# One attention kernel for a perceiver block: the value product cut into four quarters among the score chunks, with a wait on each quarter's own cast

## The chip, the cores and the metric

The kernel runs on one NeuronCore of one Trainium2 chip. The metric is the device time of one execution in microseconds (us). Engines: PE (TensorE) multiplies matrices into PSUM, DVE (VectorE) and ACT (ScalarE) read PSUM and SBUF, POOL (GpSimd) works on SBUF, SP (SyncE) here only issues transfers.

## The reference, cut to what matters

The whole block is a cross-attention with quantised operands, a self-attention and a mixture of experts, each added to `x`. The change touches the cross-attention alone. With 16 heads of 16 columns, 4,096 queries and 8,192 keys it computes

```python
q = _fq_sym(q * scale, axis=-1); k = _fq_sym(k, axis=-1); v = _fq_sym(v, axis=2)   # 8-bit grids
attn = jnp.einsum('bhqd,bhkd->bhqk', q, k)
attn = jax.nn.softmax(attn.astype(jnp.float32), axis=-1)
attn = _fq_unsigned(attn, axis=-1)          # round to 255 steps of the row's maximum
out = jnp.einsum('bhqk,bhkd->bhqd', attn, v)
```

`_fq_unsigned` divides by the row's maximum over 255, rounds, and multiplies back, so what reaches the value product are integers from 0 to 255, and a factor for each row.

## The kernel before, in words

**Units.** A unit `u` is one head and one tile of 128 queries against all 8,192 keys: 16 heads x 32 tiles = 512 units. Four units (`TG = 4`, `t` = 0 to 3) of the same head are what the code calls a head `i`: there are `HEADS` = 128 such heads. A head shares one set of keys and values and one PSUM tile `pO`.

**A unit's way through the engines.**
1. PE multiplies queries by keys into PSUM, in five chunks of 4, 3, 4, 3, 2 banks (even `t`) or 3, 4, 3, 4, 2 banks (odd `t`) of 512 columns (`scores`, L834 to L843). There are only two PSUM buffers, `ring0` and `ring1`, used in turn. The chunks with number 2 and 4 have two more matmuls ahead (L838), which are written over.
2. DVE copies each chunk to SBUF, scaled, and takes its minimum (L914: `D0` to `D4`), then reduces five minima to the bias of the exponential (L921: `BIAS`).
3. ACT takes the exponential of four pieces of 2,048 keys into 8-bit integers (L973: `E0` to `E3`).
4. SP issues a transposing transfer for each piece (L733), which brings `n_op` to `pairs`.
5. POOL casts each transposed piece to 16-bit floats, `nT` (L789, `unpack`).
6. PE multiplies `nT` by the values into `pO`, 64 matmuls of 128 columns (L853, `value_product`), done two periods after the unit's scores were read.

**What closes a head.** In the second period (`t` = 1) of the next head ACT copies the finished `pO` to `oT` (L997, `OC`), PE folds four row groups of `oT` back into `pO` (L861, `FOLD`), and in the third period (`t` = 2) ACT scales the folded result into `att_g` (L991, `FIN`, semaphore `s_fin`). The first value product of the new head writes to `pO` again, and so waits for `s_fin`: it is that of unit `t` = 0 and stands in period `t` = 2.

**What sets the order.** Each engine runs a list of steps for each period, written by hand (L645 to L647); a period `u` of PE holds chunks 2 to 4 of unit `u + 1` (`M2` to `M4`), chunks 0 and 1 of unit `u + 2` (`N0`, `N1`) and the value product of unit `u - 2` (`AV`). An engine carries out its instructions in the order of its list. Every `M` and `N` waits until DVE has emptied its PSUM buffer (`s_mu`), and DVE waits for the chunk (`s_m`). The order on ACT is `DEN E0 FIN E1 OC E2 E3`, on DVE `D0 BIAS D1 D2 D3 INV D4`, with `DEN`, `INV`, `OC`, `FOLD` at `t` = 1 and `FIN` at `t` = 2 only. In DVE's period `u`, `D0` to `D4` are the five copies of unit `u + 1`; PE's `M2` can start when `D0` is done, `M3` when `D1` is, `M4` when `D2` is, `N0` when `D3` is and `N1` when `D4` is. The semaphores that the change touches are `s_un` (a cast is done, counted four to a unit) and `s_av` (a value product is done, counted once a unit before).

Of the kernel before, what the change touches and what calls it, by code (L numbers as in the profile page):

```python
# [28 lines left out]
def build(nc, a, out):  # L29
    NT = a["x"].shape[0] * a["x"].shape[1]  # L30
    NK = a["ctx_T"].shape[1]
    QT, KT = NT // P, NK // P
    UNITS = H * QT
# [5 lines left out]
    TG = 4  # L39
# [11 lines left out]
    with top:  # L51
# [12 lines left out]
        def sem(name, ctx=top):  # L64
            return ctx.enter_context(nc.semaphore(name))
# [32 lines left out]
        with nc.Block() as block:  # L98
            @block.sync
            def _(sp):  # L100
                def weights(dst, src, s):
                    sp.dma_start(dst[:], src.rearrange("(c p) n -> p c n", p=P)).then_inc(s, 16)
                weights(wkv_sb, a["L0_xattn_Wkv"], s_wkv)
                sp.wait_ge(s_zero, 1)
                for r in range(PARTS):
                    sp.dma_start(b_all[32 * r:32 * r + 1, 0:2 * D],
                                 a["L0_xattn_bkv"].rearrange("(a n) -> a n", a=1)).then_inc(s_bkv, 16)
                    sp.dma_start(b_all[32 * r:32 * r + 1, 2 * D:3 * D],
                                 a["L0_xattn_bq"].rearrange("(a n) -> a n", a=1)).then_inc(s_bkv, 16)
# [529 lines left out]
        NE = 4  # L639
        EW = NK // NE  # L640
        EK = KT // NE
        EP = EK // 2
        PAIRS = KT // 2
        HEADS = NG * H
        PE_STEPS = "M2 M3 AV0 M4 AV1 N0 N1 FOLD".split()  # L645
        DVE_STEPS = "D0 BIAS D1 D2 D3 INV D4".split()
        ACT_STEPS = "DEN E0 FIN E1 OC E2 E3".split()  # L647

# [37 lines left out]
        s_un = sem("integers_unpacked", xs)  # L686
        s_av = sem("value_product_done", xs)
# [9 lines left out]
        def scored(u, j):  # L697
            return u * NM + j + 1

        def exped(u, j):  # L700
            return u * NE + j + 1

        def ge(e, s, value):

            if not isinstance(value, int) or value > 0:
                e.wait_ge(s, value)
# [12 lines left out]
        def exists(u):  # L719
            return not isinstance(u, int) or 0 <= u < UNITS  # L720

        with nc.Block() as block:
# [19 lines left out]
            @block.gpsimd  # L742
            def _(pool):
                def load_keys(g, h, b):
                    cols = bass.ds(g * TG * P, TG * P)
                    pool.dma_start(k_op[b][0:KR, :], kT_d[h * KR:(h + 1) * KR, :]).then_inc(s_k[b], 16)
                    for r in range(PARTS):
                        pool.dma_start(q_op[b][r * HD:(r + 1) * HD, :], qT_d[h * HD:(h + 1) * HD, cols]  # L748
                                       ).then_inc(s_qh[b], 16)

                def load_values(h, b):
                    pool.dma_start(v_st[b][:], v_d[h]).then_inc(s_v[b], 16)

                def stage_steps(g, h):
                    nc.gpsimd.tensor_copy(step[h % 2][:], q_step[:, bass.ds(g * TG + h * QT, TG)]).then_inc(s_st, 1)

                def stage_values(b):
                    nc.gpsimd.tensor_copy(v_op[b][:, :, 0:HD], v_st[b][:].rearrange("p (k d) -> p k d", d=HD)
                                          ).then_inc(s_vo, 1)

                def values(i, b, h, more):
                    pool.wait_ge(s_v[b], (i + 2 - b) * 8)
                    ge(pool, s_av, (i - 1) * TG)
                    pool.sem_inc(s_turn, 1)
                    stage_values(b)
                    if more:
                        pool.wait_ge(s_vo, i + 1)
                        pool.sem_inc(s_turn, 1)
                        load_values((h + 2) % H, b)

                def keys(g, h, i):
                    pool.wait_ge(s_mu, scored((i - 2) * TG + TG - 1, NM - 1))
                    stage_steps(g, h)
                    load_keys(g, h, h % 2)

                def store(g):
                    pool.wait_ge(s_fin, (g + 1) * H)
                    pool.sem_inc(s_turn, 1)
                    pool.dma_start(att_d[bass.ds(g, 1)].rearrange("a p t d -> (a p) t d"), att_g[:]).then_inc(s_as, 16)

                def unpack(u, t, j):
                    par = t % 2
                    pool.wait_ge(s_n[par][j], (u + 2 - par) * 8)
                    if j == 0:
                        ge(pool, s_av, u - 1)
                    pool.sem_inc(s_turn, 1)
                    src = pairs[par][:, j * EP:(j + 1) * EP, :].rearrange("p a b -> p (a b)").bitcast(U8).rearrange(
                        "p (a b c) -> p a c b", c=2, b=P)
                    nc.gpsimd.tensor_copy(nT[par][:, j * EK:(j + 1) * EK, :].rearrange("p (a c) b -> p a c b", c=2), src  # L789
                                          ).then_inc(s_un, 1)  # L790

                def head(g, h, i):
                    for t in range(TG):
                        u = i * TG + t
                        unpack(u, t, 0)
                        if t == 3 and exists(u + 2 * TG):
                            keys(g + (h + 2) // H, (h + 2) % H, i + 2)
                        unpack(u, t, 1)
                        if t == 3 and h == 0 and exists(u - H * TG):
                            store(g - 1)  # L800
                        unpack(u, t, 2)
                        unpack(u, t, 3)
                        if t == 1 and (not isinstance(i, int) or 2 <= i + 1 < HEADS):
                            values(i + 1, (h + 1) % 2, (h + 1) % H, exists(u + 3 * TG))

                for b in range(2):
                    nc.gpsimd.memset(v_op[b][:], 0.0).then_inc(s_init, 1)
                stage_steps(0, 0)
                stage_steps(0, 1)
                pool.wait_ge(s_pad, 2)  # L810
                load_keys(0, 0, 0)
                load_values(0, 0)
                load_keys(0, 1, 1)
                load_values(1, 1)
                pool.wait_ge(s_init, 2)
                for b in range(2):
                    pool.wait_ge(s_v[b], 16)
                    stage_values(b)
                for b in range(2):
                    pool.wait_ge(s_vo, b + 1)  # L820
                    load_values(2 + b, b)
                for h in range(H):
                    head(0, h, h)
                with pool.Fori(1, NG - 1) as g:
                    for h in range(H):
                        head(g, h, g * H + h)
                for h in range(H):
                    head(NG - 1, h, (NG - 1) * H + h)
                store(NG - 1)
                pool.wait_ge(s_as, 16 * NG)  # L830

            @block.tensor
            def _(pe):
# [8 lines left out]
                                              k_op[b][:, at + n * BANK:at + (n + 1) * BANK], start=True, stop=True)  # L842
                    mm.then_inc(s_m, 1)  # L843

                def value_product(u, i, b, t, half):

                    if half == 0:
                        pe.wait_ge(s_un, (u + 1) * NE)
                    if half == 0 and t == 0:
                        pe.wait_ge(s_vo, i + 1)  # L850
                        ge(pe, s_fin, i)
                    for n in range(half * KT // 2, (half + 1) * KT // 2):
                        mm = nc.tensor.matmul(pO[32 * (n % CG):32 * (n % CG) + 32, t, :], v_op[b][:, n, :],  # L853
                                              nT[t % 2][:, n, :], start=n < CG, stop=n >= KT - CG)
                    if half == 1:
                        mm.then_inc(s_av, 1)

                def fold_groups(i):
                    pe.wait_ge(s_oc, i + 1)
                    for t in range(TG):  # L860
                        mm = nc.tensor.matmul(pO[:, t, 0:HD], oT[:, t, :], fold[:], start=True, stop=True)  # L861
                    mm.then_inc(s_of, 1)

                def period(i, hp, t):
                    u = i * TG + t
                    for x in PE_STEPS:
                        if x[0] in "MN":
# [31 lines left out]
                    for t in range(TG):  # L899
                        period(HEADS - 2 + hp, hp, t)  # L900
                for t in range(TG - 2, TG):
                    for half in range(2):
                        value_product(UNITS - TG + t, HEADS - 1, 1, t, half)
                fold_groups(HEADS - 1)

            @block.vector
# [57 lines left out]
            def _(act):  # L964
# [27 lines left out]
                    last.then_inc(s_fin, 1)  # L992

                def copy_products(i):
                    act.wait_ge(s_av, i * TG + TG)
                    ge(act, s_of, i)
                    nc.scalar.copy(oT[:], pO[:]).then_inc(s_oc, 1)  # L997

# [534 lines left out]
        NE = a["member"].shape[0] // PARTS  # L1533
# [297 lines left out]
```

## Time and profile before

| | |
|---|---|
| Three executions | 6421.8, 6457.5 and 7106.4 us, median 6457.5 us |
| The profiled execution | 6431.7 us, span of its trace 6430.2 us |
| Stage of the cross-attention (first to last chunk of scores) | some 340 to 5,190 us of the span |
| Busy over the whole span | DVE 87%, ACT 74%, POOL 71%, PE 70% |

What comes ahead of and behind that stage (keys, values and queries; then projection, self-attention and experts) is not touched by the change.

### The profile page before, as it was taken

To read this page: it belongs to the slowest core of one execution; us is meant where nothing else is said; L and a number is where in the kernel's file an instruction comes from. 1 tells how busy PE (TensorE), PEld (TensorE's weight loads), DVE (VectorE), ACT (ScalarE), POOL (GpSimd) and SP (SyncE) were. 2 spreads that over 40 slices of the span, in tenths; PEclk is the share of its full clock that TensorE was granted. 3 is DMA by queue.
4 is the path that set the end of the run, shared out by engine and by line. 5 is a ranking of instruction groups with operands and counts; after the bars stand their busy time and mean duration, and the time that the engine had idled before them with its cause. 6 is when DMAs were issued, how large, how long until landed. Compare 5 with 4: busy or idle time off the path is not lost. (4 is left out here: it accounts for less than half of the span.)

```text
span 6430.2 us, 141911 instructions
## 1 busy us (share of the span) xinstructions
PE 4487.4 (70%) x48939; PEld 2136.5 (33%) x49654; DVE 5619.6 (87%) x7587; ACT 4772.4 (74%) x6550; POOL 4588.0 (71%) x3259
## 2 busy tenths in 40 slices
PE   7556666666666666666666666666666646769999
PEld 3322222222222222222222222232222233455555
DVE  8799999999999999999999999999999936872222
ACT  5479998998999899989999988989989933331111
POOL 4578888888898888888888888888888823420000
PEclk9899999999999999999999999999999978979999
DMA  4267777777777777777777777777777730010000
GB/s 127 76 123 139 140 142 146 139 144 142 142 143 141 143 139 141 142 140 140 142 142 145 139 138 139 147 140 141 145 141 141 138 87 0 0 36 4 7 8 9
DMA packets 2231984, 735.80 MB, mean 114 GB/s; under 512 B 2175781, under 2 KB 2209416, under 8 KB 2225577
## 3 DMA queue, kind: packets, MB, share of 16 engines
q1 hardware_dynamic: 2196265, 576.08, 44.0%
q0 software_dynamic: 35456, 157.33, 13.8%
q14 instruction: 234, 1.92, 0.1%
q8 instruction: 29, 0.48, 0.0%
HBM read 168.97 MB, written 27.26 MB: 31 GB/s over the span
## 5 line engine op out<-in xcount | busy, mean ns | idle before, releaser
L914 DVE TENSOR_SCALAR_CACHE_REDUCE scores<-ring,step 128x2048 f32<-128x2048 f32 (+2 forms) x2560 | 4780.0, 1918 | 50.5 <-PE ring L841 38.1
L973 ACT ACTIVATE n_op<-scores,bias 128x2048 uint8<-128x2048 f32 x2048 | 4076.2, 1997 | 284.6 <-DVE m_rest L921 284.5
L789 POOL CAST nT<-pairs 128x2048 f16<-128x2048 uint8 x2048 | 3791.1, 1890 | 510.9 <-DMA pairs<-n_op 491.4
L841 PE MATMUL ring<-x_all,q_op 128*128 128x512 bf16 x7746 | 2147.6, 385 | 702.2 <-DVE scores L914 630.5
L841 PEld LDWEIGHTS ring<-x_all,q_op 128*128 128x128 bf16 x8192 | 682.2, 98 | 1854.1 <-DVE scores L914 1180.6
L838 PE MATMUL ring<-x_all,q_op 128*128 128x512 bf16 x1793 | 571.9, 389 | 775.2 <-DVE scores L914 744.1
L853 PE MATMUL pO<-nT,v_op 128*32 128x128 f16 x32768 | 659.0, 223 | 141.0 <-ACT att_g L991 109.0
L853 PEld LDWEIGHTS pO<-nT,v_op 128*32 128x32 f16 x32768 | 481.6, 98 | 590.2 <-issue 512.2
L838 PEld LDWEIGHTS ring<-x_all,q_op 128*128 128x128 bf16 x2048 | 116.7, 97 | 997.8 <-DVE scores L914 979.4
L973 ACT ACTIVATION_READ_ACCUMULATOR n_op<-scores,bias 128x1 f32 x2048 | 396.1, 193 | 0.0
L1752 DVE TENSOR_TENSOR h_up<-h_gate,pUp 128x512 f32<-128x512 f32 x112 | 76.9, 687 | 298.8 <-ACT h_gate L1741 298.8
L1741 ACT ACTIVATE h_gate<-pGt 128x512 f32<-128x512 f32 x112 | 66.8, 597 | 337.7 <-PE pWt L1715 337.6
L1342 POOL TENSOR_TENSOR k_bd<-kT,head_mask 128x512 f32<-128x512 f32 x128 | 129.3, 1042 | 166.7 <-ACT kT L1442 166.7
L997 ACT COPY oT<-pO 128x512 f32<-128x512 f32 x128 | 74.9, 585 | 221.9 <-PE pO L853 221.9
L1712 PE MATMUL pGt<-zT,wg_sb 128*128 x448 | 223.0, 620 | 2.8 <-DVEq L1747 2.8
L1712 PE MATMUL pUp<-zT,wu_sb 128*128 x448 | 211.1, 594 | 0.0
L914 DVE DVE_READ_ACCUMULATOR scores<-ring,step 128x1 f32 x2560 | 209.3, 82 | 0.0
L1724 PE MATMUL pDn<-wd_sb,hidden 128*128 128x256 f32 (+1 forms) x896 | 195.6, 380 | 0.0
L748 POOL DMA_DIRECT2D q_op<-queries_transposed x384 | 188.6, 495 | 2.0 <-issue 1.8
L1724 PEld LDWEIGHTS pDn<-wd_sb,hidden 128*128 128x128 f32 (+1 forms) x896 | 169.5, 190 | 24.8 <-issue 1.8
L1768 DVE TENSOR_TENSOR x_all<-x_all,pDn 128x256 f32 x32 | 13.5, 421 | 169.6 <-PE pDn L1724 169.6
L1741 ACT ACT_TABLE_LOAD x8 | 10.3, 1283 | 200.6 <-PE pWt L1715 200.6
(202 smaller groups left out, 3616.1 us busy)
## 6 DMA issues: line engine op xcount, KB each, us to landing
x_all<-keys_transposed POOLq DMA_DIRECT2D x128, 768.0 KB, 8.5
v_st<-value_integers POOLq DMA_DIRECT2D x128, 256.0 KB, 3.5
pairs<-n_op SPq DMA_TRANSPOSE x2048, 2.8
keys_transposed<-kT_s POOLq DMA_DIRECT2D x32, 384.0 KB, 3.3
cT<-in_ctx_T SPq DMA_DIRECT2D x32, 256.0 KB, 2.6
x_all<-in_x SPq DMA_DIRECT2D x2, 4096.0 KB, 16.2
q_op<-queries_transposed POOLq DMA_DIRECT2D x384, 16.0 KB, 8.4
value_integers<-v_int SPq DMA_DIRECT2D x1, 4096.0 KB, 13.0
```

The source lines that it names most:

```text
L748: pool.dma_start(q_op[b][r * HD:(r + 1) * HD, :], qT_d[h * HD:(h + 1) * HD, cols]).then_inc(s_qh[b], 16)
L789: nc.gpsimd.tensor_copy(nT[par][:, j * EK:(j + 1) * EK, :].rearrange("p (a c) b -> p a c b", c=2), src).then_inc(s_un, 1)
L838: nc.tensor.matmul(slot(t, j)[:, n * BANK:(n + 1) * BANK], q_op[b][:, t * P:(t + 1) * P], k_op[b][:, at + n * BANK:at + (n + 1) * BANK], s ...
L841: mm = nc.tensor.matmul(slot(t, j)[:, n * BANK:(n + 1) * BANK], q_op[b][:, t * P:(t + 1) * P], k_op[b][:, at + n * BANK:at + (n + 1) * BAN ...
L853: mm = nc.tensor.matmul(pO[32 * (n % CG):32 * (n % CG) + 32, t, :], v_op[b][:, n, :], nT[t % 2][:, n, :], start=n < CG, stop=n >= KT - CG)
L914: nc.vector.tensor_scalar(score[t % 2][:, at:at + width * BANK], slot(t, j)[:, 0:width * BANK], step[b][:, t:t + 1], None, ALU.mult, ALU.m ...
L973: nc.scalar.activation(n_op[par][:, j * EW:(j + 1) * EW], score[par][:, j * EW:(j + 1) * EW], ACT.Exp, bias=bias[par][:], scale=-1.0, accu ...
L1342: nc.gpsimd.tensor_tensor(k_bd[i][:, c, b], kT[i][:, c, b * B:(b + 1) * B].unsqueeze(1).to_broadcast([P, HC, B]), head_mask[:].unsqueeze(2 ...
L1712: nc.tensor.matmul(dst[0:r, :], w[:, c, cols], zT[:, c, bass.ds(blk * TB, TB), :].rearrange("p t n -> p (t n)"), start=c == 0, stop=c == D ...
L1724: mm = nc.tensor.matmul(pDn[t % 2], hidden[0:rows[f], f, t * P:(t + 1) * P], wd_sb[0:rows[f], f, :], start=f == 0, stop=f == NF - 1)
L1741: nc.scalar.activation(h_gate[f % 2][0:rows[f], :], pGt[f % 2][0:rows[f], :], ACT.Silu).then_inc(s_si, 1)
L1752: nc.vector.tensor_tensor(h_up[i][0:rows[f], :], h_gate[i][0:rows[f], :], pUp[i][0:rows[f], :], ALU.mult).then_inc(s_hu, 1)
```

## The change

The value product of a unit is cut into four quarters of 16 matmuls (16 of 64 key tiles) instead of two halves of 32, and PE's list of steps puts one quarter behind each of `M2`, `M3`, `M4` and `N0`. Each quarter waits for the cast of its own piece, where before the first half waited for all four casts. Each quarter adds one to `s_av`, so all thresholds on `s_av` are multiplied by four. Each cast now waits for the quarter of unit `u - 2` that read the same piece of the same buffer, where before only the first cast waited, for the whole product of `u - 2`. The wait for `s_fin` and for the staged values stays with the first quarter of unit `t` = 0.

```diff
-        PE_STEPS = "M2 M3 AV0 M4 AV1 N0 N1 FOLD".split()
+        PE_STEPS = "M2 AV0 M3 AV1 M4 AV2 N0 AV3 N1 FOLD".split()
...
-                    ge(pool, s_av, (i - 1) * TG)
+                    ge(pool, s_av, (i - 1) * TG * NE)
...
-                    if j == 0:
-                        ge(pool, s_av, u - 1)
+                    ge(pool, s_av, exped(u - 2, j))
...
-                def value_product(u, i, b, t, half):
-
-                    if half == 0:
-                        pe.wait_ge(s_un, (u + 1) * NE)
-                    if half == 0 and t == 0:
+                def value_product(u, i, b, t, j):
+                    pe.wait_ge(s_un, exped(u, j))
+                    if j == 0 and t == 0:
                         pe.wait_ge(s_vo, i + 1)
                         ge(pe, s_fin, i)
-                    for n in range(half * KT // 2, (half + 1) * KT // 2):
+                    for n in range(j * EK, (j + 1) * EK):
                         mm = nc.tensor.matmul(pO[32 * (n % CG):32 * (n % CG) + 32, t, :], v_op[b][:, n, :],
                                               nT[t % 2][:, n, :], start=n < CG, stop=n >= KT - CG)
-                    if half == 1:
-                        mm.then_inc(s_av, 1)
+                    mm.then_inc(s_av, 1)
...
-                    act.wait_ge(s_av, i * TG + TG)
+                    act.wait_ge(s_av, (i * TG + TG) * NE)
```

The lines of the kernel after are up to four lower than before: L838, L841, L853 and L861 of PE become L837, L840, L850 and L857, and L997 of ACT becomes L993.

**PE in the third period of a head (`t` = 2).** The rows below are PE's instructions from the fold to chunk `N0`, in the kernel before; the names in brackets are semaphores waited for (`head_finished` is `s_fin`, `scores_copied` is `s_mu`, `integers_unpacked` is `s_un`).

```order
L861 MATMUL pO<-fold,oT 128x16 x3
L838 MATMUL ring<-x_all,q_op 128x512 [waits scores_copied]
L841 MATMUL ring<-x_all,q_op 128x512 x3
L841 MATMUL ring<-x_all,q_op 128x512 [waits scores_copied]
L841 MATMUL ring<-x_all,q_op 128x512 x3
L850 REGISTER_ALU [waits integers_unpacked]
L853 MATMUL pO<-nT,v_op 32x128 [waits head_finished,head_values_staged]
L853 MATMUL pO<-nT,v_op 32x128 x31
L838 MATMUL ring<-x_all,q_op 128x512 [waits scores_copied]
```

The same place in the kernel after:

```order
L857 MATMUL pO<-fold,oT 128x16 x3
L837 MATMUL ring<-x_all,q_op 128x512 [waits scores_copied]
L840 MATMUL ring<-x_all,q_op 128x512 x3
L847 REGISTER_ALU [waits integers_unpacked]
L850 MATMUL pO<-nT,v_op 32x128 [waits head_finished,head_values_staged]
L850 MATMUL pO<-nT,v_op 32x128 x15
L840 MATMUL ring<-x_all,q_op 128x512 [waits scores_copied]
L840 MATMUL ring<-x_all,q_op 128x512 x3
L850 MATMUL pO<-nT,v_op 32x128 [waits integers_unpacked]
```

The matmul that waits for `head_finished` has moved from behind chunk `M3` (the second row of L841 with a wait) to ahead of it.

**PE in the second period of a head (`t` = 1).** The rows below are PE's instructions from chunk `M4` to the fold, before:

```order
L838 MATMUL ring<-x_all,q_op 128x512 [waits scores_copied]
L841 MATMUL ring<-x_all,q_op 128x512 x2
L853 MATMUL pO<-nT,v_op 32x128 x32
L841 MATMUL ring<-x_all,q_op 128x512 [waits scores_copied]
L841 MATMUL ring<-x_all,q_op 128x512 x2
L841 MATMUL ring<-x_all,q_op 128x512 [waits scores_copied]
L841 MATMUL ring<-x_all,q_op 128x512 x3
L861 MATMUL pO<-fold,oT 128x16 [waits head_products_copied]
```

and after:

```order
L837 MATMUL ring<-x_all,q_op 128x512 [waits scores_copied]
L840 MATMUL ring<-x_all,q_op 128x512 x2
L850 MATMUL pO<-nT,v_op 32x128 [waits integers_unpacked]
L850 MATMUL pO<-nT,v_op 32x128 x15
L840 MATMUL ring<-x_all,q_op 128x512 [waits scores_copied]
L840 MATMUL ring<-x_all,q_op 128x512 x2
L850 MATMUL pO<-nT,v_op 32x128 [waits integers_unpacked]
L850 MATMUL pO<-nT,v_op 32x128 x15
L840 MATMUL ring<-x_all,q_op 128x512 [waits scores_copied]
L840 MATMUL ring<-x_all,q_op 128x512 x3
L857 MATMUL pO<-fold,oT 128x16 [waits head_products_copied]
```

The last matmuls of the value product stood ahead of chunk `N0` before and stand behind it now, between `N0` and `N1`.

## Rows read from the trace of the kernel before

**Rows 1.** Busy time by stretch: us, PE, PEld, DVE, ACT, POOL, PEclk, DMA share, GB/s.

```profile
1000.00:5000.00 4000.00, 2701.13 (x35921) 1173.60 (x36503) 3964.76 (x5199) 3606.16 (x4777) 3525.87 (x2446) 0.99 0.74 142
```

**Rows 2.** The page's costliest groups, DVE's copy of a chunk with its idle time.

```profile
L914 DVE TENSOR_SCALAR_CACHE_REDUCE scores<-ring,step 128x2048 f32<-128x2048 f32 (+2 forms) x2560 | 4780.0, 1918 | 50.5 <-PE ring L841 38.1
```

**Rows 3.** Waits over the whole span: total us, times, longest us.

```profile
ACT oT L997 <- PE pO L853: 221.9, 128, 7.4
PE pO L853 <- ACT att_g L991: 109.0, 126, 1.3
```

**Rows 4.** Waits between 1000 and 5000 us: total us, times, longest us.

```profile
PE pO L853 <- ACT att_g L991: 90.6, 105, 1.3
DVE scores L914 <- PE ring L841: 24.7, 46, 3.1
PE pO L853 <- POOL nT L789: 13.9, 10, 3.8
DVE scores L914 <- ACT n_op L973: 8.6, 5, 1.8
POOL nT L789 <- PE pO L853: 5.8, 6, 2.5
```

**Rows 5.** Timeline of DVE, copies of one head's period t = 2.

```profile
2521.71 1.81 DVE L914 TENSOR_SCALAR_CACHE_REDUCE scores<-ring,step 128x1536 f32<-128x1536 f32 x1
...
2523.44 2.35 DVE L914 TENSOR_SCALAR_CACHE_REDUCE scores<-ring,step 128x2048 f32<-128x2048 f32 x1
...
2525.72 1.28 DVE L914 TENSOR_SCALAR_CACHE_REDUCE scores<-ring,step 128x1024 f32<-128x1024 f32 x1
```

**Rows 6.** Timeline of PE in the same head, periods t = 1 and t = 2.

```profile
2515.72 0.63 PE L853 MATMUL pO<-nT,v_op 128*32 128x128 f16 x32
2516.49 0.82 PE L841 MATMUL ring<-x_all,q_op 128*128 128x512 bf16 x3
...
2519.94 0.81 PE L841 MATMUL ring<-x_all,q_op 128*128 128x512 bf16 x3
2521.85 1.04 PE L841 MATMUL ring<-x_all,q_op 128*128 128x512 bf16 x4 [1.10 <-DVE scores L914]
2523.74 0.63 PE L853 MATMUL pO<-nT,v_op 128*32 128x128 f16 x32 [0.86 <-ACT att_g L991]
2524.30 0.60 PE L838 MATMUL ring<-x_all,q_op 128*128 128x512 bf16 x2
```

**Rows 7.** Timeline of ACT in the same head.

```profile
2516.40 0.58 ACT L997 COPY oT<-pO 128x512 f32<-128x512 f32 x1 [1.60 <-PE pO L853]
2516.88 2.00 ACT L973 ACTIVATE n_op<-scores,bias 128x2048 uint8<-128x2048 f32 x1
...
2522.85 0.75 ACT L991 ACTIVATE att_g<-pO,rden 128x16 f32<-128x16 f32 x4
```

**Rows 8.** Timeline of POOL in the same head.

```profile
2510.93 15.03 POOL L789 CAST nT<-pairs 128x2048 f16<-128x2048 uint8 x8 [0.35 <-DMA pairs<-n_op]
2525.92 1.03 POOL L758 COPY v_op<-v_st 128x1024 f16<-128x1024 f16 x1
```

**Rows 9.** Timeline of PE ahead of and in two stretches of low clock.

```profile
2160.08 0.60 PE L838 MATMUL ring<-x_all,q_op 128*128 128x512 bf16 x2 [2.50 <-DVE scores L914]
...
2162.43 1.89 PE L841 MATMUL ring<-x_all,q_op 128*128 128x512 bf16 x4 [0.75 <-DVE scores L914]
...
3203.51 1.04 PE L841 MATMUL ring<-x_all,q_op 128*128 128x512 bf16 x4 [1.10 <-DVE scores L914]
3205.40 1.04 PE L853 MATMUL pO<-nT,v_op 128*32 128x128 f16 x32 [0.86 <-ACT att_g L991]
```

**Rows 10.** Busy time by stretch of 1 us, columns as in the first group.

```profile
3204.00:3205.00 1.00, 0.55 (x3) 0.05 (x1) 1.00 (x1) 1.00 (x6) 1.00 (x1) 1.00 1.13 258
...
3206.00:3207.00 1.00, 1.00 (x21) 0.46 (x11) 1.00 (x1) 1.00 (x1) 1.00 (x1) 0.50 1.14 258
```

**Rows 11.** Timeline of DVE, copies that waited for PE behind those stretches.

```profile
2164.36 2.35 DVE L914 TENSOR_SCALAR_CACHE_REDUCE scores<-ring,step 128x2048 f32<-128x2048 f32 x1 [0.25 <-PE ring L841]
...
3208.31 1.28 DVE L914 TENSOR_SCALAR_CACHE_REDUCE scores<-ring,step 128x1024 f32<-128x1024 f32 x1 [0.85 <-PE ring L841]
...
3210.07 2.35 DVE L914 TENSOR_SCALAR_CACHE_REDUCE scores<-ring,step 128x2048 f32<-128x2048 f32 x1 [0.47 <-PE ring L841]
```

More of the change, by code:

```diff
@@ L901, in _ @@
                 for t in range(TG - 2, TG):
-                    for half in range(2):
-                        value_product(UNITS - TG + t, HEADS - 1, 1, t, half)
+                    for j in range(NE):
+                        value_product(UNITS - TG + t, HEADS - 1, 1, t, j)
                 fold_groups(HEADS - 1)
```

## The prediction

> **What bounds the kernel now.** I read the busy times by stretch first. Between 1000 and 5000 us, deep in the cross-attention, DVE is busy 3964.8 of 4000 us (99.1%), ACT 3606.2 (90%), POOL 3525.9 (88%), PE 2701.1 (68%) [rows 1]. DVE sets the pace; its copies of score chunks stand one behind the other. Its whole idle time ahead of them is 50.5 us in the span [rows 2]. So whatever the change saves on another engine can return at most some 50 us (0.8%), while each microsecond for which DVE lacks a chunk is added to the time in full.
>
> The waits come next, for the places where PE isn't waiting for DVE. In 4000 us PE waited 13.9 us for casts and 90.6 us, in 105 waits, for ACT's last step of the previous head [rows 4]. That second wait is the one to look at: over the span it comes 126 times, 109.0 us in total, 0.87 us each, at most 1.3 [rows 3], so in practically each head after the first, of the same length each time. Today it costs nothing, and the timeline shows why. In one head ACT's FIN starts at 2522.85 and ends at 2523.60 [rows 7], and the value product of unit t = 0 starts at 2523.74 after 0.86 us of idle PE [rows 6]. The chunk ahead of it, M3, had been written from 2521.85 on [rows 6], while DVE copied M2's (2521.71 to 2523.44), so DVE took M3's at 2523.44 without a gap [rows 5].
>
> **The change, part by part.**
>
> *Each quarter waits for its own cast.* PE's waits for casts are 13.9 us of 4000 [rows 4], and they lie in PE's free time. In the head shown eight casts (units t = 0 and t = 1) run from 2510.93 to 2525.92, so the four of unit t = 0 end near 2518.4 [rows 8], and its product starts at 2523.74: a margin of 5.3 us. Cost and gain zero; what hides it is DVE's queue of copies. Were this cover gone, the price would be the 13.9 us.
>
> *Each cast waits for its quarter.* The casts waited 5.8 us for products [rows 4]. POOL has three more waits a unit, with the later casts and behind them SP's transfers queued after each. The quarters of u - 2 are issued within one period and the casts of u follow later, so I take zero. POOL is idle 12% of the stretch, which is 4.5 us in a head of some 38 us (4000/105).
>
> *Splitting the products.* 32 matmuls take 0.63 us [rows 6], so there are as many matmuls as before, in four portions of at most 0.4 us. In periods without the FIN wait a portion lies between two chunks, where PE idles 1 us or more on DVE (1.10 us ahead of M3 [rows 6]). Nothing on the path. What relief it brings ahead of N0 is bounded by DVE's 24.7 us of waits for PE [rows 4].
>
> *The last quarter moves behind N0.* In period t = 1 the product ended at 2515.72 + 0.63 = 2516.35 and ACT's copy OC of `pO` started at 2516.40, having waited 1.60 us for it [rows 6, 7]. Now the last quarter follows N0, which starts at 2516.49, since it needs DVE's D3, and takes 0.82 [rows 6]: 2517.31. A value product directly behind a chunk begins about when the chunk ends; sixteen matmuls take between half of 0.63 and 0.4, I take 0.33. So the product ends at 2517.64 and OC starts at 2517.69, **1.29 us later**. Queued behind OC on ACT are E2, E3, E0 of the next unit and FIN. Before, FIN ended 2523.60 - 2516.40 = 7.20 us after OC's start, with no idle time between [rows 7]. So FIN now ends at 2524.89.
>
> *The first quarter moves ahead of M3.* PE's order is fixed, so M3 now queues behind the quarter that waits for FIN. M2 ends at 2519.94 + 0.81 = 2520.75; PE then stands still until the quarter starts at 2524.89 + 0.14 = 2525.03 (the 0.14 is 2523.74 - 2523.60 [rows 6, 7]), that is 4.28 us. The quarter takes 0.33, M3 starts at 2525.36 and with its 1.04 us ends at 2526.40. DVE takes it 0.04 us later, as 2164.36 follows 2162.43 + 1.89 [rows 9, 11]. DVE would start D3 at 2526.44 instead of 2523.44: **3.00 us lost in each head**. M4, next, has its 2.28 us (2523.44 to 2525.72 [rows 5]) under D3; it needs some 0.3 for the second quarter and 1.0 for itself, so nothing more is lost. In the next head ACT waits for DVE's bias again at t = 1 and OC for PE, so the loss repeats: 127 heads x 3.00 = 381 us.
>
> *PE's clock.* PE stands still for 4.3 us in each head, longer than the idle times at which its clock fell before. At 3203.51 to 3205.40 it had waited 1.10 us, written M3 and waited 0.86 us [rows 9]; then the granted clock went from 1.00 (2.4 GHz) to 0.50 (1.2 GHz) [rows 10], and DVE lost 0.85 + 0.47 = 1.32 us [rows 11]. After an idle 2.50 us at 2160 the same came, and a chunk of four took 1.89 us instead of 1.04 [rows 9]. Where the low clock meets M3, the loss is that difference, 0.85 us; it is then hidden partly behind D3's 2.28 us. Bounds: 0 (no fall, or before M3) and 1.70 (two chunks lengthened, each by 0.85). I take 0.85 in each head, since the idle stretch ends exactly at M3: 127 x 0.85 = 108 us.
>
> The Trainium skill bears on this (TensorE: Matmul & The Clock Gate, section on HAM oscillation): a kernel that idles on a wait between bursts of matmuls can start each burst at the low clock, and pays at every repetition. By its figures of 426.7 and 215.7 ns for a matmul of 512 columns at the two levels, M3 would grow by 0.84 us, an estimate of 107 us in 127 heads. Rows so far show the fall only now and then, since the idle times were shorter.
>
> **The sum.** 6431.7 (the profiled execution) + 381 + 108 = 6921 us, say **6920**. The profiled execution lies 0.4% under the median of the three shown, 6457.5, and by it the change is +7.6%.
>
> **The rivals.**
> - *The stall alone, without a lower clock.* 6431.7 + 381 = 6813 us. For it: a clock of 0.99 in the stage [rows 1]. Against it: falls after shorter idle times [rows 9, 10].
> - *OC is not later.* If ACT's copy came when it did before, FIN would end at 2523.60, M3 would start at 2523.74 + 0.33 = 2524.07, DVE would get it at 2525.15, 1.71 us late: 127 x 1.71 = 217, giving 6649 us. Against it: OC waited 221.9 us in 128 heads for PE [rows 3], so it follows PE.
> - *Slow clock that costs more.* 3.00 + 1.70 = 4.70 us in each head, 597 us, 7029 us.
> - *Not slower: FIN comes in time.* DVE loses nothing if M3 is written by 2523.40, so the quarter must start by 2523.40 - 1.04 - 0.33 = 2522.03 and FIN end by 2521.9, that is 3.0 us earlier than I work out and 1.7 earlier than in the trace of before. ACT would have to get OC that much earlier, and it waits for PE there. Then only relief is left: 6431.7 less at most 50.5 [rows 2], 6381 to 6432 us, no change by measure.
>
> **How the numbers follow.** Stall with low clock 0.54 (6920), stall alone 0.24, costlier clock 0.09, OC not later 0.07, not slower 0.05, and 0.01 for a gain over 2%, for which no row speaks. The range goes down to the stall alone less all of DVE's present idle time, 6813 - 50 = 6763, say 6765, and up to 7029, say 7030. About 2% is what a measurement of this kernel can tell from no change; all cases but the last two lie beyond it, so slower has 0.94, within 2% 0.05, faster 0.01.
>
> **What the changed profile would show.** DVE waits for PE at its copies, one wait of 3 to 4 us a head, some 400 to 500 us in all where 38.1 stood. PE waits for ACT's FIN some 127 times, about 4.3 us each instead of 0.87, directly ahead of the quarter, with M3 behind it. OC on ACT starts right after the quarter behind N0. A head takes 41 to 42 us, and DVE's busy share falls to about 90%. PE's granted clock is 0.5 right after the stall in most heads if the clock term is right, near 1 if the stall-alone rival is. The forecast is wrong if the wait for FIN stays near 0.9 us, or if DVE's copies stay without gaps while PE waits.

## The result, and the profile after

The kernel after takes 6932.4 us (median of four, 6931.3 to 6939.7), the kernel before 6445.7 (median of three, 6421.8 to 6457.5; a fourth execution, at 7106.4 us, was disturbed and is left out). The ratio is 1.076, 95% interval 1.0725 to 1.0803: 7.6% slower. Over the 13 to 20 runs of before that stand beside each group of experiments its median is 6436 to 6442 us, and the terms below are taken against 6440. A difference between experiments of different groups can be off by those 5 us.

The profiled execution of after has a span of 6938.2 us. The stretch from 1000 to 5000 us in it (columns as in rows 1):

```profile
1000.00:5000.00 4000.00, 2606.54 (x32465) 1102.58 (x33039) 3597.41 (x4711) 3273.80 (x4322) 3212.00 (x2216) 0.93 0.66 128
```

DVE is busy 89.9% of it, where it was 99.1% [rows 1], and PE's mean granted clock is 0.93 where it was 0.99. The work hasn't grown; DVE has gaps. The page's group of DVE's copies says how much and behind what:

```profile
L910 DVE TENSOR_SCALAR_CACHE_REDUCE scores<-ring,step 128x2048 f32<-128x2048 f32 (+2 forms) x2560 | 4789.9, 1918 | 549.8 <-PE ring L840 537.9
```

Idle time ahead of the copies is 549.8 us instead of 50.5 [rows 2], 499 us more, which is the lengthening within 2%. The waits over the whole span (total us, times, longest):

```profile
PE pO L850 <- ACT att_g L987: 545.3, 127, 4.3
...
DVE scores L910 <- PE ring L840: 537.9, 160, 11.1
```

PE waits for FIN 127 times as before, but 4.29 us each instead of 0.87 [rows 3]. In one head PE's timeline shows M2 (2502.89), the standstill, the first quarter and M3 behind it:

```profile
2502.89 0.81 PE L840 MATMUL ring<-x_all,q_op 128*128 128x512 bf16 x3
2508.00 0.51 PE L850 MATMUL pO<-nT,v_op 128*32 128x128 f16 x16 [4.29 <-ACT att_g L987]
2508.44 1.89 PE L840 MATMUL ring<-x_all,q_op 128*128 128x512 bf16 x4
```

ACT's timeline in the same head has OC, which waits longer for the product than the 1.60 us of before [rows 7], and FIN:

```profile
2500.65 0.59 ACT L993 COPY oT<-pO 128x512 f32<-128x512 f32 x1 [2.90 <-PE pO L850]
...
2507.11 0.75 ACT L987 ACTIVATE att_g<-pO,rden 128x16 f32<-128x16 f32 x4
```

and DVE's has the gap ahead of its copy of M3's chunk, where it had none [rows 5]:

```profile
2510.36 2.35 DVE L910 TENSOR_SCALAR_CACHE_REDUCE scores<-ring,step 128x2048 f32<-128x2048 f32 x1 [3.88 <-PE ring L840]
```

Last, the clock around the standstill (columns as in rows 1, the granted clock is third from the right):

```profile
2507.00:2508.00 1.00, 0.00 (x2) 0.04 (x2) 0.00 (x0) 1.00 (x7) 1.00 (x1) 1.00 0.76 169
2508.00:2509.00 1.00, 1.00 (x18) 0.52 (x19) 0.00 (x0) 1.00 (x1) 0.92 (x2) 0.58 0.51 117
2509.00:2510.00 1.00, 1.00 (x4) 0.15 (x1) 0.00 (x0) 1.00 (x3) 1.00 (x1) 0.50 0.65 145
```

PE stands still at 1.00, and the clock falls to 0.50 (1.2 GHz) as the quarter and M3 begin. So M3 takes 1.89 us instead of 1.04. The pattern repeats in each head; this one's OC comes again 41.27 us later, at 2541.92.

This head is one of the cheaper ones, since the clock fell during its quarter. From 1000 to 5000 us the trace shows 96 quarters behind such a wait; 84 of them ran wholly at the low clock (0.61 or 0.62 us), and DVE's usual gap is 4.0 us. One such head, in PE's and DVE's timelines:

```profile
2590.65 0.62 PE L850 MATMUL pO<-nT,v_op 128*32 128x128 f16 x16 [4.29 <-ACT att_g L987]
2591.20 1.89 PE L840 MATMUL ring<-x_all,q_op 128*128 128x512 bf16 x4
...
2593.13 2.35 DVE L910 TENSOR_SCALAR_CACHE_REDUCE scores<-ring,step 128x2048 f32<-128x2048 f32 x1 [3.99 <-PE ring L840]
```

### The profile page after: what moved, and what is told of

The parts are those of the page before. It is cut to its first block and busy times, and to the rows that moved or that the text cites. A ratio compares the mean times of both kernels' runs of the same rounds, so it can differ in the third digit from the quotient of the medians.

```text
span 6938.2 us, 144882 instructions
## 1 busy us (share of the span) xinstructions
PE 4711.2 (68%) x48877; PEld 2191.9 (32%) x49654; DVE 5630.6 (81%) x7587; ACT 4782.8 (69%) x6550; POOL 4612.0 (66%) x3259
## 3 DMA queue, kind: packets, MB, share of 16 engines
q14 instruction: 242, 1.97, 0.1%
## 5 line engine op out<-in xcount | busy, mean ns | idle before, releaser
L910 DVE TENSOR_SCALAR_CACHE_REDUCE scores<-ring,step 128x2048 f32<-128x2048 f32 (+2 forms) x2560 | 4789.9, 1918 | 549.8 <-PE ring L840 537.9
L840 PE MATMUL ring<-x_all,q_op 128*128 128x512 bf16 x7560 | 2198.3, 401 | 523.2 <-DVE scores L910 440.7
L850 PE MATMUL pO<-nT,v_op 128*32 128x128 f16 x32768 | 891.1, 233 | 556.9 <-ACT att_g L987 545.3
L837 PE MATMUL ring<-x_all,q_op 128*128 128x512 bf16 x1917 | 625.3, 403 | 822.3 <-DVE scores L910 802.4
L840 PEld LDWEIGHTS ring<-x_all,q_op 128*128 128x128 bf16 x8192 | 704.9, 101 | 1321.0 <-DVE scores L910 542.5
L850 PEld LDWEIGHTS pO<-nT,v_op 128*32 128x32 f16 x32768 | 512.2, 100 | 1503.3 <-issue 1298.4
L837 PEld LDWEIGHTS ring<-x_all,q_op 128*128 128x128 bf16 x2048 | 118.3, 99 | 1070.0 <-DVE scores L910 1044.5
L993 ACT COPY oT<-pO 128x512 f32<-128x512 f32 x128 | 75.1, 587 | 374.6 <-PE pO L850 374.6
L1764 DVE TENSOR_TENSOR x_all<-x_all,pDn 128x256 f32 x32 | 13.5, 421 | 169.6 <-PE pDn L1720 169.6
```

The source lines that it names most:

```text
L837: nc.tensor.matmul(slot(t, j)[:, n * BANK:(n + 1) * BANK], q_op[b][:, t * P:(t + 1) * P], k_op[b][:, at + n * BANK:at + (n + 1) * BANK], s ...
L840: mm = nc.tensor.matmul(slot(t, j)[:, n * BANK:(n + 1) * BANK], q_op[b][:, t * P:(t + 1) * P], k_op[b][:, at + n * BANK:at + (n + 1) * BAN ...
L910: nc.vector.tensor_scalar(score[t % 2][:, at:at + width * BANK], slot(t, j)[:, 0:width * BANK], step[b][:, t:t + 1], None, ALU.mult, ALU.m ...
```

## The experiments

Theory: the FIN wait now stands ahead of M3 and comes later, and PE's standstill brings on a low clock that lengthens M3. The rivals: only the place of the wait counts; the low clock costs nothing of its own; or finer waits and smaller portions cost the time. All edits but one are to the kernel after. Where steps of PE differ by period, the loop takes `PE_AT.get(t, PE_STEPS)` in place of `PE_STEPS`.

### The place of the wait

```diff
+        PE_AT = {2: "M2 M3 AV0 AV1 M4 AV2 N0 AV3 N1 FOLD".split()}
```

> The changed kernel, with one chunk moved in the third period of a head only (t = 2): PE's steps are M2 M3 AV0 AV1 M4 ..., so M3 no longer queues behind the wait for FIN. The last quarter stays behind N0 at t = 1, so FIN still ends 1.29 us late. Theory (queue behind the FIN wait): M3 is on time, but two quarters stand between the FIN wait and M4. They start at 2525.03 on the clock of the head of before and take 0.66, M4 with its two extra matmuls 1.0, so D4 is 0.95 us late in each head: 127 x 0.95 = 121 us, some 6555 us; with a low clock behind the now shorter stand of PE (2.1 us) up to 0.9 us more a head, 6670. Rival (the finer waits or the splitting themselves cost the time): stays near 6930. Rival (moving the FIN wait is everything, the late OC nothing): back to 6430 to 6450.

Measured: 6723.3 us, ratio to before 1.0442 (1.0419 to 1.0465). M3 no longer queues, and 209 us come back, but the time is 53 us above the upper end expected. DVE's gaps differ from head to head. In one head:

```profile
2501.56 1.28 DVE L911 TENSOR_SCALAR_CACHE_REDUCE scores<-ring,step 128x1024 f32<-128x1024 f32 x1 [1.41 <-PE ring L841]
...
2503.92 2.35 DVE L911 TENSOR_SCALAR_CACHE_REDUCE scores<-ring,step 128x2048 f32<-128x2048 f32 x1 [1.07 <-PE ring L841]
```

and in the next:

```profile
2540.97 1.28 DVE L911 TENSOR_SCALAR_CACHE_REDUCE scores<-ring,step 128x1024 f32<-128x1024 f32 x1 [0.88 <-PE ring L841]
```

The 0.88 us is the order's (0.95 expected); the other head lost 2.48 us. The clock in it had fallen:

```profile
2501.00:2502.00 1.00, 1.00 (x18) 0.35 (x16) 0.44 (x1) 1.00 (x3) 1.00 (x2) 0.50 0.00 0
```

The low clock meets more than one chunk here, and the expectation of at most 0.9 us for it was too small. A later run with fillers takes most of the clock's share out.

### The late OC

```diff
+        PE_AT = {1: "M2 AV0 M3 AV1 M4 AV2 AV3 N0 N1 FOLD".split()}
```

> The changed kernel, with the last quarter back ahead of N0 in the second period only (t = 1: ... M4 AV2 AV3 N0 N1), so that OC and FIN come as early as before; the FIN wait stays ahead of M3. Theory: FIN ends 1.29 us earlier than in the changed kernel, PE stands 3.0 us instead of 4.3, DVE's gap is 1.71 us plus the clock term of 0 to 0.9: 6431.7 + 217 = 6649 to 6760 us, so 165 to 280 us faster than the changed kernel. Rival (only the place of the FIN wait counts): unchanged, 6930.

Measured: 6787.5 us, 1.0545 (1.0522 to 1.0569). It is 145 us faster than the kernel after, less than the 165 to 280 expected (the run with seven fillers below says why), so the late OC has a share and the rival "only the place counts" falls. PE's wait for FIN in it:

```profile
PE pO L851 <- ACT att_g L988: 379.8, 127, 3.0
```

2.99 us each, 1.30 less than the 4.29 of after: OC's delay arrives at FIN in full, as worked out (1.29).

### Both

```diff
+        PE_AT = {1: "M2 AV0 M3 AV1 M4 AV2 AV3 N0 N1 FOLD".split(),
+                 2: "M2 M3 AV0 AV1 M4 AV2 N0 AV3 N1 FOLD".split()}
```

> Both edits of the two runs before: last quarter ahead of N0 at t = 1, and FIN wait behind M3 at t = 2; quarters, their own waits and the casts' waits stay everywhere, and the interleaved order stays at t = 0 and t = 3. Theory: nothing of the loss is left, 6420 to 6450 us, within 0.5% of the kernel before. Rival (finer waits, splitting): clearly slower than before, by more than 1%.

Measured: 6419.1 us, 0.9967 (0.9958 to 0.9977). A few portions moved by one place, in two of four periods, give back 513 us. Quarters, waits and the interleaved order elsewhere stay, so they don't cost the time.

### The clock

```diff
+                            if x == "AV0" and t == 2:
+                                pe.wait_ge(s_mu, scored(u + 1, 3 - RING))
+                                for n in range(12):
+                                    nc.tensor.matmul(slot(3, 3)[:, 0:BANK], q_op[hp][:, 3 * P:4 * P],
+                                                     k_op[hp][:, 0:BANK], start=True, stop=True)
```

> The changed kernel with 12 matmuls of 512 columns more in the third period (t = 2), after M2 and before the wait for FIN, written to M3's own buffer once DVE has emptied it, and written over by M3. They keep PE busy for 2.6 us of the 4.3 in which it stood still and end before FIN does. Theory with a clock term: the granted clock stays 1.0 around M3, M3 takes 1.04 instead of 1.89 us, DVE's gap falls from 3.9 to 3.0 us, and the time from 6932 to some 6825 us (127 x 0.85 = 108 less). Rival (the low clock is only beside the stall and costs nothing): 6932, gap 3.9. Rival (fillers are in the way of the quarter): slower than 6932.

Measured: 6787.1 us, 1.0543 (1.052 to 1.0566): 145 us less than the kernel after by adding 127 x 12 matmuls. PE's timeline has the fillers, a short wait for FIN, the quarter and M3 at 1.04 us:

```profile
2520.31 2.76 PE L877 MATMUL ring<-x_all,q_op 128*128 128x512 bf16 x12 [1.10 <-DVE scores L916]
2523.51 0.41 PE L851 MATMUL pO<-nT,v_op 128*32 128x128 f16 x16 [0.43 <-ACT att_g L993]
2523.84 1.04 PE L841 MATMUL ring<-x_all,q_op 128*128 128x512 bf16 x4
```

DVE's gap in this head is that of the stall alone, 3.00 us in the prediction, and from 1000 to 5000 us 99 gaps are 2.9 to 3.0 us long:

```profile
2524.92 2.35 DVE L916 TENSOR_SCALAR_CACHE_REDUCE scores<-ring,step 128x2048 f32<-128x2048 f32 x1 [2.92 <-PE ring L841]
```

and the stage runs at 1.00:

```profile
1000.00:5000.00 4000.00, 2913.30 (x35214) 1195.54 (x35207) 3699.64 (x4850) 3370.59 (x4452) 3303.59 (x2283) 1.00 0.68 132
```

So the clock is a cause of its own, 145 / 127 = 1.14 us a head. Most of it is the difference between the usual gaps of the two runs, 4.0 and 2.92 us.

### The first two edits with fillers

The first edit with six fillers ahead of the FIN wait:

```diff
+        PE_AT = {2: "M2 M3 AV0 AV1 M4 AV2 N0 AV3 N1 FOLD".split()}
...
+                            if x == "AV0" and t == 2:
+                                pe.wait_ge(s_mu, scored(u + 1, 4 - RING))
+                                for n in range(6):
+                                    nc.tensor.matmul(slot(3, 4)[:, 0:BANK], q_op[hp][:, 3 * P:4 * P],
+                                                     k_op[hp][:, 0:BANK], start=True, stop=True)
```

> The first experiment (FIN wait behind M3 at t = 2, OC late) with 6 matmuls more ahead of the FIN wait, written to M4's own buffer once DVE has emptied it, and written over by M4. In the first experiment DVE lost 1.41 + 1.07 us in a head whose clock had fallen and 0.88 us in one whose clock had not. Theory: with PE kept busy only the 0.9 us a head is left: 6420 (quarters without the stall) + 127 x 0.9 = 6535 us. Rival (the surplus of the first experiment over its forecast comes from the order, not the clock): stays near 6723.

Measured: 6566.4 us, 1.0196 (1.0172 to 1.0219). Against 6723.3 that is 157 us less, nearly all of the 168 by which the first experiment lay above its 6555. What is left, 146 us over 6420 or 1.15 us a head, lies above the 0.9. DVE's gaps tell why: from 1000 to 5000 us 85 are 0.9 us long, as forecast for the order, and 16 are 2.4 to 2.5. Six fillers didn't hold the clock in every head. In a head with the long gap it fell just after they had begun, and they took 2.48 instead of 1.47 us. FIN had ended at 1738.12 there and the quarters began at 1739.23, so the slow fillers stood in the way. PE's timeline, the clock and DVE's timeline (the profile calls the releaser of DVE's copy "remote" in this run; the copy is that of M4's chunk):

```profile
1736.82 2.48 PE L877 MATMUL ring<-x_all,q_op 128*128 128x512 bf16 x6 [0.70 <-DVE scores L916]
...
1738.00:1739.00 1.00, 1.00 (x4) 0.15 (x1) 1.00 (x2) 1.00 (x2) 0.93 (x2) 0.50 0.15 35
...
1741.43 1.28 DVE L916 TENSOR_SCALAR_CACHE_REDUCE scores<-ring,step 128x1024 f32<-128x1024 f32 x1 [2.40 <-remote]
```

So the order costs 0.9 us a head, and the rest is the clock that still fell in about one head of six, with the fillers slowed by it.

The second edit with seven fillers, placed as in the experiment on the clock:

```diff
+        PE_AT = {1: "M2 AV0 M3 AV1 M4 AV2 AV3 N0 N1 FOLD".split()}
...
+                            if x == "AV0" and t == 2:
+                                pe.wait_ge(s_mu, scored(u + 1, 3 - RING))
+                                for n in range(7):
...
```

> The second experiment (last quarter ahead of N0 at t = 1, FIN wait ahead of M3) with 7 matmuls more ahead of the FIN wait, written to M3's buffer once it is empty, and written over by M3. Theory: without low clock the gap is 1.71 us a head: 6420 + 217 = 6637 us; against the changed kernel with fillers (6787) that is 150 us or 1.2 us a head, the share of the late OC (1.29 forecast). Rival (OC's delay is absorbed on ACT): near 6787.

Measured: 6620.2 us, 1.028 (1.0256 to 1.0303). DVE's gap in a head:

```profile
2500.69 2.35 DVE L916 TENSOR_SCALAR_CACHE_REDUCE scores<-ring,step 128x2048 f32<-128x2048 f32 x1 [1.63 <-PE ring L841]
```

1.63 us, where the early FIN was worked out to leave 1.71. And 6787.1 - 6620.2 = 167 us is the late OC alone, 1.31 us a head. The same run tells why the second experiment fell short: without fillers that order took 6787.5 us, so there the clock cost 167 us, 1.32 a head, where at most 0.9 had been allowed. In it 216 waits of DVE for PE stand in 127 heads, in this run 133.

### FIN earlier on ACT

```diff
-        ACT_STEPS = "DEN E0 FIN E1 OC E2 E3".split()
+        ACT_STEPS = "DEN FIN E0 E1 OC E2 E3".split()
```

> The changed kernel's order on PE, with FIN on ACT one exponential earlier (ahead of E0 of the third period, t = 2). Theory: FIN ends 1.99 us earlier, M3 starts at 2523.37 on the clock of the head of before and DVE's gap falls from 3.0 to 1.0 us; with the clock term of 0 to 0.9: 6431.7 + 127 x 1.0 = 6560 to 6675 us. It gives the slope: each microsecond that FIN comes earlier is one microsecond a head. Rival (the wait for FIN isn't what stops M3): unchanged, 6930.

Measured: 6640.3 us, 1.0311 (1.0288 to 1.0335). 292 us come back for an exponential's 1.99 us: 2.3 us a head, since the clock's share changes too. The slope is read from the trace, in a head where the quarter (0.41 us) and M3 (1.04 us) ran at full clock:

```profile
2500.61 0.41 PE L850 MATMUL pO<-nT,v_op 128*32 128x128 f16 x16 [2.31 <-ACT att_g L987]
...
2502.02 2.35 DVE L910 TENSOR_SCALAR_CACHE_REDUCE scores<-ring,step 128x2048 f32<-128x2048 f32 x1 [0.95 <-PE ring L840]
```

PE's wait is 1.98 us shorter than the 4.29 of after, and the gap is 1.97 us shorter than the 2.92 with fillers: a microsecond for a microsecond.

FIN two exponentials earlier, at the end of the second period:

```diff
-        ACT_STEPS = "DEN E0 FIN E1 OC E2 E3".split()
+        ACT_STEPS = "DEN E0 E1 OC E2 FIN E3".split()
...
-                        elif t == 2 and exists(i - 1) and x == "FIN":
+                        elif t == 1 and exists(i - 1) and x == "FIN":
```

> The changed kernel with FIN on ACT moved to the second period, between E2 and E3 (t = 1), right after PE's fold can be done. PE's order is that of the changed kernel everywhere. Theory: FIN ends near 2520.95 on the clock of the head of before, about when M2 ends (2520.75), so the first quarter no longer waits and M3 comes in time: the whole loss is gone, 6400 to 6450 us. If fewer stands of PE also mean fewer falls of its clock, up to 35 us below the kernel before. Rival (interleaved quarters delay chunks by themselves): above 6450, DVE still with gaps in each head.

Measured: 6399.7 us, 0.9935 (0.9918 to 0.9952), faster than both kernels. PE's order is that of the kernel after, OC still waits 2.90 us for the last quarter, and the loss of 533 us is gone. PE's wait for FIN shrinks to a third of a microsecond, and M3 is in time:

```profile
2510.31 0.41 PE L850 MATMUL pO<-nT,v_op 128*32 128x128 f16 x16 [0.33 <-ACT att_g L987]
2511.08 1.04 PE L840 MATMUL ring<-x_all,q_op 128*128 128x512 bf16 x4 [0.36 <-DVE scores L910]
```

In the stage DVE is busy 99.8% of the time and the clock is at 1.00:

```profile
1000.00:5000.00 4000.00, 2866.70 (x36768) 1175.11 (x36768) 3990.74 (x5240) 3619.85 (x4812) 3553.14 (x2464) 1.00 0.73 143
```

The same move of FIN in the kernel before, with its old order:

> The kernel before, with FIN on ACT moved to the second period, between E2 and E3, as in the run before this one. It tells what the earlier FIN brings with the old order. Theory: PE's wait of 0.87 us a head for FIN goes, but it lay in free time: within 0.5% of before, at best 35 us less where it prevents a fall of the clock. OC isn't moved. Beside it the run before shows whether the quarters bring anything of their own once the FIN wait is out of the way: the theory says less than 0.3%.

Measured: 6414.2 us, 0.996 (0.9945 to 0.9975), 26 us less than before. With FIN out of the way the whole change (order, quarters and finer waits together) is worth 14 us, 0.2%, under the 0.3% expected. What the order alone is worth there no run shows.

### The finer waits

```diff
-        PE_STEPS = "M2 AV0 M3 AV1 M4 AV2 N0 AV3 N1 FOLD".split()
+        PE_STEPS = "M2 M3 AV0 AV1 M4 AV2 AV3 N0 N1 FOLD".split()
```

> The changed kernel's quarters and waits, in the order of before: PE's steps are M2 M3 AV0 AV1 M4 AV2 AV3 N0 N1, so only the semaphores differ from the kernel before (each quarter waits for its own cast, each cast for its own quarter). Theory: these waits cost and bring nothing, since DVE is busy 99% of the stage: within 0.3% of before. The range for a gain ends at DVE's idle 50 us, 0.8%. Rival (earlier casts and products give slack that shortens the time): 0.3 to 0.8% faster. Rival (more semaphores cost): slower by over 0.3%.

Measured: 6419.6 us, 0.9967 (0.9956 to 0.9978): a small gain. Which of the two kinds of waits brings it was asked with two more runs; their diffs are shown against this one. In the first the casts wait as before:

```diff
-                    ge(pool, s_av, exped(u - 2, j))
+                    if j == 0:
+                        ge(pool, s_av, (u - 1) * NE)
```

> Quarters' own waits on PE alone: order of before (M2 M3 AV0 AV1 M4 AV2 AV3 N0 N1), each quarter waits for its own cast, but the first cast of a unit waits for the whole product of u - 2, as before. The run with both kinds of finer waits was 0.33% faster than before. If the finer waits on PE bring it: again 0.3%, some 6420 us. If those on POOL bring it: as before, 6440.

Measured: 6418.4 us, 0.9967 (0.9954 to 0.998). In the second the products wait as before:

```diff
-                    pe.wait_ge(s_un, exped(u, j))
+                    if j == 0:
+                        pe.wait_ge(s_un, (u + 1) * NE)
```

> The casts' own waits alone: order of before, the first quarter waits for all four casts as before, but each cast waits only for the quarter of u - 2 that read its piece. If these bring the 0.33%: some 6420 us; if those on PE do: 6440. Both near 6420 would say that it is neither, but what they share: more semaphore instructions on PE, or quarters instead of halves.

Measured: 6451.7 us, 1.0018 (1.0005 to 1.0031). So the gain belongs to the quarters' waits on PE; the casts' waits bring nothing and may cost a little. Quarters in place of halves are in all three runs, and so not the cause.

## Why the prediction was right, point by point

**What bounds the kernel.** Right. The time grew by DVE's added idle time (499 us of gaps, 492 us over 6440), although PE, ACT and POOL all have more free time than before.

**The wait that was free and would not stay so.** Right, and shown from both sides: the FIN wait back behind M3 with OC back in place gives 6419 us, and FIN out of the way with the order kept gives 6400.

**OC 1.29 us later.** Right. PE's wait for FIN differs by 1.30 us and the times with fillers by 1.31 us a head.

**3.00 us of stall a head, 381 us.** Right. PE stood 4.29 us (4.28 worked out). With the clock held up, DVE's gap is 2.9 to 3.0 us in 99 heads of the stage, and the time is 367 us over the run with the new waits in the old order (6787.1 - 6419.6), 2.89 a head.

**The clock, 0.85 us a head, 108 us.** The mechanism was right, the size too small: 145 us, 1.14 a head. The step took one lengthened chunk, M3, and left out the quarter between the standstill and M3, which runs at the low clock too. M3 grew by just 0.85 (1.89 against 1.04), and the quarter by 0.21 in most heads (0.62 against 0.41): 1.06 of the 1.14. The rest is a later copy that waits again in some heads: DVE waits 160 times for PE, with the clock held up 130 times. In one such head the clock was at 0.50 from 2631 to 2638 us, twice as long as in the head shown first:

```profile
2634.51 2.35 DVE L910 TENSOR_SCALAR_CACHE_REDUCE scores<-ring,step 128x2048 f32<-128x2048 f32 x1 [4.00 <-PE ring L840]
...
2638.64 2.35 DVE L910 TENSOR_SCALAR_CACHE_REDUCE scores<-ring,step 128x2048 f32<-128x2048 f32 x1 [0.48 <-PE ring L840]
```

The value lies within the bounds given, 0 and 1.70.

**Splitting at zero.** Right: with both edits the quarters stay and the time is 6419 us. The reading beneath it was too generous, though. The 1.10 us of idle PE stands ahead of M3; ahead of N1 it is 0.45 us in the same head of before.

**Finer waits at zero.** Off by a little: 21 us, 0.33%, was gained where zero was taken. The step priced PE's waits for casts as free because they lie in PE's idle time. On the whole they do, but not all. Over the span PE's waits for casts are 31.7 us before, 13.5 with PE's finer waits alone, 18.1 with both kinds and 44.3 with POOL's alone; DVE's waits for PE go the same way, 38.1, 22.4, 25.9 and 47.0 us. That agrees with the times, though each is one trace, and it doesn't account for all of the 21 us.

**The sum.** Against before: + 367 for the stall, + 145 for the clock, - 21 for the finer waits, 491 us; measured 492. The forecast of 6920 had 381, 108 and 0, so the measured terms differ from it by - 14, + 37 and - 21, which nearly cancel; most of the 12 us of miss is its base, 6431.7 where 6440 was the usual time. That the miss is so small is luck and flatters the terms. This split depends on the base: against the kernel with FIN moved (6399.7), whose stage ran at a mean clock of 1.00 with DVE's gaps gone, the stall is 387 us or 3.05 a head.

**The rivals.** The stall alone (6813) is close to what the fillers made of it (6787). "OC is not later" (6649) answers to 6620, the second edit with fillers. "FIN comes in time" gave its time of 6381 to 6432 with 6400, once FIN was moved. The costlier clock (7029) took 1.70 us a head for the clock, where 1.14 was measured.

**What the profile would show.** Right on the standstill (127 waits of 4.29 us), the length of a head (41.27 us) and DVE's busy share (89.9%). DVE's waits for PE, 400 to 500 us forecast, are 537.9.

The Trainium skill (TensorE: Matmul & The Clock Gate, section on HAM oscillation) says that a kernel idling between bursts of matmuls can start every burst at the low clock. The trace agrees: in 84 of 96 heads the quarter behind the standstill ran wholly at 1.2 GHz. M3 grew by 0.85 us where the estimate from the page's figures was 0.84. What that estimate leaves out is mainly the quarter ahead of M3.

## What to carry to other kernels

An in-order engine's wait that is free today is free because of what stands ahead of it; before moving it, work out when its releaser comes and what will queue behind it. Look also for what the same change does to the releaser: here a portion moved one place later delayed the wait's own release by 1.3 us, and moved one place earlier made that wait count. When a new standstill of PE recurs, price the slower clock behind it as well, and before giving up a good order, try moving the releaser: one step of ACT made the new order the fastest of all, if only by 14 us over the old order with the same step.

## What the runs showed of the hardware

Adding matmuls made the kernel faster: 12 fillers in each of 127 heads took 145 us off, since the granted clock stayed at 1.00 in place of 0.93 in the stage. In the run with six fillers, behind waits of 1.10 and 0.70 us, the clock still fell in about one head of six, and the six matmuls then took up to 2.7 us instead of 1.47.

In six neighbouring heads of the kernel after (2500 to 2720 us) PE's standstill has the same 4.3 us, but the clock fell at different points of it. By the mean clock of stretches of 1 us it fell 0.2 us behind the end of the standstill in the first head, 0.1, 0.6 and 1.0 us ahead of the end in the next three, and 2.1 and 2.7 us ahead in the last two. In the first three it then stayed at 0.50 for over 3 us, in the other three for nearly 7. Falls come after shorter standstills too: with FIN ahead of E0, PE stood 2.31 us a head, and the quarter behind it ran wholly at the low clock in some 40 heads of the stage and at full clock in 54. What decides when it falls and for how long these runs don't tell.
